# Two graph layers over one streamed adjacency: each engine's order written out call by call, with 12 input checks on VectorE

## The chip, the cores and the metric

The kernel runs on one NeuronCore of one Trainium2 chip. The metric is device time in microseconds, the median over runs of the same program. Beside those runs stands one profiled execution, from which every row below comes; its span starts at the first recorded instruction and ends at the last.

## The reference, cut to what matters

```python
def _L0_gnn_ref(x, adj, W, a):
    Wh = x @ W
    e = leaky_relu((Wh @ a[:128])[:, None] + (Wh @ a[128:])[None, :], 0.2)
    mask = (adj > 0) | eye(4096)
    alpha = softmax(where(mask, e, NEG_INF), axis=1)
    return alpha @ Wh

def _L1_gnn_ref(z, dist_matrix, W, B):
    sens = exp(-(1.0 / dist_matrix - 1.0) ** 2 / 0.5)
    return where(dist_matrix < 1.0, sens, 0.0) @ (z @ W + B)

h = relu(layernorm(x));  x = x + _L0_gnn_ref(h, adj, W0, a0)
h = relu(layernorm(x));  x = x + _L1_gnn_ref(h, adj, W1, B1)
```

`x` is 4096 x 128 and `adj` is 4096 x 4096, both float32, so `adj` is 67 MB. Its entries are 0 or 1 and most are 0; edges are dense only among the first nodes. With entries of 0 and 1 the second layer adds nothing: a 0 gives exp of minus infinity, a 1 fails the cutoff. The kernel relies on that, checks it for every entry, and has a general path (a branch behind a flag) for any other input.

## The kernel before

**Work in chunks.** `adj` is read in 32 chunks of 2 MB (128 partitions x 16384 bytes), numbered 0 to 31. Eight chunks, in two halves of four column blocks, make up one *super* of 1024 rows; there are four supers. The chunks go through a ring of six buffers (`adj_ring`). SyncE issues all loads (line 347); the load of chunk i waits until chunk i - 6 has been packed, has been turned where that is needed, and has been checked (lines 358 to 369).

**What is done to a chunk.**
- *check* (VectorE line 1035, or ScalarE lines 866 and 869): every entry is 0 or 1. `DVE_CHECKED` names the chunks that VectorE checks with one pass (13 of them), `ACT_CHECKED` those that ScalarE checks with two passes (19). Chunk 31 is VectorE's.
- *pack* (TensorE lines 560, 567 and 573): matmuls fold the adjacency bits of eight rows and the column number into one float word in PSUM (`bank`). The two chunks 2n and 2n+1 share *step* n and its PSUM banks. Blocks on the diagonal come from `clean`, written by `clean_diagonal` on VectorE (line 1051).
- *scan* (VectorE line 1065): the largest 8 words of each segment of a packed step go to `cand`, after both chunks of the step are packed.
- *turn_hub*, *turn_columns*, *hub*, *column* handle the first 128 nodes and the first 128 columns, which are dense, with weights for all pairs instead of a list of edges. `add_columns(s)` (TensorE line 670) starts the sums of super s in PSUM.

**Edges.** The 16 steps are cut into five *pieces* (steps 0-3, 4-7, 8-11, 12-14, 15). After the last scan of piece n, VectorE runs `pick(n)` (line 1078 on), TensorE `place(n)` (lines 629 and 636), VectorE `decode(n)` (line 1181 on, node numbers to `index`) and `pick_shared(n)` (line 1108 on), TensorE `place_shared(n)` (line 646), VectorE `decode_shared(n)` (line 1145 on, to `shared_index`). GpSimd then fetches one row of `node_table` per partition and slot with an indirect DMA (line 478), 76 in all, in 11 *groups* g over a ring of four. For each group VectorE computes edge weights with `weigh(g)` (lines 1222 to 1251, to `spread`), and TensorE adds the weighted rows into the sums with `scatter(g)` (line 682). `add_self(s)` (line 677) adds each node itself, scaled beforehand by ScalarE (`scale_self`, line 889). `epilogue(s)` (VectorE lines 1313 and 1319) divides and adds to `x_sb`; SyncE stores it. The sums of all supers use the same PSUM banks, so `add_columns(s)` waits for `epilogue(s - 1)`. `row_scores` (TensorE line 601) and `row_weights` (ScalarE line 878) prepare each super's row factors, in two halves.

**The end.** `judge` (VectorE lines 1335 to 1340) waits for ScalarE's last check and stands ahead of `weigh(10)`; `count_bad` (TensorE line 699) and `raise_flag` (ScalarE line 895) turn the verdicts into the flag. Then `scatter_last` and `last_epilogue` end the kernel in three parts.

**What sets the order.** There is no scheduler: each engine executes its instructions in the order of its block and waits on semaphores. Before the change each block loops over the chunks and takes from tables at which chunk a call is made:

```python
PICK_AT = {8: 0, 16: 1, 24: 2, 30: 3}
WEIGH_AT = {13: 0, 15: 1, 17: 2, 20: 3, 22: 4, 25: 5, 28: 6}
SCATTER_AT = {14: 0, 16: 1, 18: 2, 21: 3, 23: 4, 26: 5, 29: 6, 30: 7}
EPILOGUE_AT = {19: 0, 27: 1}
```

So `scan(n)` stands at chunk 2n + 2 on VectorE, `place(n)` ahead of the pack of the chunk in `PICK_AT`, and so on; the end of VectorE's block is `epilogue(2)`, `scan(15)`, `pick(4)`, `pick_shared(4)`, `decode_shared(4)`, `check(31)`, `weigh(8)`, `weigh(9)`, `judge()`, `weigh(10)`, `last_epilogue()`.

## Time and profile before

| what | us |
|---|---|
| runs of the kernel: median (lowest, highest of 3) | 255.73 (254.72, 261.86) |
| the profiled execution's own time | 253.61 |
| its span | 251.8 |
| busy: TensorE / VectorE / ScalarE / GpSimd | 170.7 / 186.3 / 188.1 / 120.9 |

The profiled execution takes 1.8 us outside its span. In the rows, PE is TensorE's matmuls, DVE is VectorE, ACT is ScalarE, POOL is GpSimd and SP is SyncE; L and a number is the line of the kernel. A number in brackets behind a timeline row is how long the engine sat idle before it, with what ended that wait ("remote" and "issue" name nothing the profile could identify). An f32 matmul is recorded as two instructions, so a `scatter` of 8 matmuls counts x16. The ends of matmuls are modelled, and a few records can be missing.

### The profile page before, as it was taken

How to read it: one execution, taken by the hardware profiler on the slowest of the kernel's cores; microseconds unless marked ns; L12 is line 12 of the kernel's file. 1: busy time of each engine (PE TensorE's matmuls, PEld its weight loads, DVE VectorE, ACT ScalarE, POOL GpSimd, SP SyncE). 2: the span in 40 equal slices, each digit the busy share in tenths (PEclk: the TensorE clock that was granted, in tenths of full speed). 3: DMA queues.
4: the chain of work that ended last, by engine and by line, in shares of the span. 5: the costliest groups of instructions: out<-in, count | busy, mean ns of one | idle time of the engine just before them, and what ended most of it. 6: DMA issues, size and time to landing. Idle time of an engine off the chain costs nothing. (4 is left out here: it accounts for less than half of the span.)

```text
span 251.8 us, 3251 instructions
## 1 busy us (share of the span) xinstructions
PE 170.7 (68%) x970; PEld 118.5 (47%) x970; DVE 186.3 (74%) x563; ACT 188.1 (75%) x201; POOL 120.9 (48%) x131
## 2 busy tenths in 40 slices
PE   0296797595149849794999787557494929557390
PEld 0295553253135525563576554434353626356390
DVE  7967949989988799999599993865317581067963
ACT  0899876977993089899983999999999999900000
POOL 0395040000007798987689898137760027713810
PEclk9999999979557986999599999797887776965778
DMA  5999999999999999999999999999994001120002
GB/s 160 389 410 411 407 410 415 422 411 408 409 409 405 390 394 395 403 394 395 392 393 401 398 391 397 390 408 389 384 392 187 0 5 40 26 85 0 9 10 90
DMA packets 22389, 76.96 MB, mean 306 GB/s; under 512 B 2643, under 2 KB 3255, under 8 KB 22368
## 3 DMA queue, kind: packets, MB, share of 16 engines
q1 hardware_dynamic: 18912, 71.31, 72.5%
q0 software_dynamic: 3040, 5.34, 6.3%
q8 instruction: 9, 0.15, 0.2%
q10 hardware_dynamic: 416, 0.07, 0.2%
q14 instruction: 12, 0.10, 0.1%
HBM read 74.52 MB, written 4.28 MB: 313 GB/s over the span
## 5 line engine op out<-in xcount | busy, mean ns | idle before, releaser
L478 POOL DMA_INDIRECT gathered_rows<-node_table,index x48 | 68.1, 1418 | 73.2 <-issue 45.2
L573 PE MATMUL bank<-adj_ring,pack_w 128*128 128x512 bf16 (+3 forms) x262 | 73.9, 411 | 5.4 <-DVE clean L1051 2.9
L866 ACT ACTIVATE trash_a<-adj_ring,below_one 128x4096 fp8e4<-128x4096 f32 x19 | 70.4, 3705 | 4.3 <-DMA adj_ring<-in_adj 3.3
L869 ACT ACTIVATE trash_a<-adj_ring 128x4096 fp8e4<-128x4096 f32 x19 | 68.7, 3618 | 0.6
L1035 DVE SCALAR_TENSOR_TENSOR trash_v<-adj_ring 128x4096 fp8e4<-128x4096 f32 x13 | 57.3, 4411 | 0.1
L478 POOL DMA_INDIRECT gathered_rows<-node_table,shared_index x28 | 37.7, 1345 | 17.6 <-DVE shared_index L1156 9.4
L573 PEld LDWEIGHTS bank<-adj_ring,pack_w 128*128 128x128 bf16 x262 | 27.3, 107 | 37.7 <-issue 17.6
L682 PE MATMUL bank<-gathered_rows,spread 128*128 128x129 f32 x176 | 27.3, 321 | 8.9 <-DVE spread L1233 8.6
L1065 DVE MAX8 cand<-bank 128x8 f32<-128x120 f32 (+24 forms) x82 | 23.3, 349 | 11.5 <-PE bank L573 8.0
L682 PEld LDWEIGHTS bank<-gathered_rows,spread 128*128 128x128 f32 x176 | 25.9, 233 | 10.2 <-issue 9.9
L895 ACT ACTIVATE bad_terms<-bank 1x48 f32<-1x48 f32 x1 | 0.2, 200 | 22.7 <-PE bank L699 22.7
L878 ACT ACTIVATE r_rows<-bank 128x512 f32<-128x512 f32 x8 | 4.6, 590 | 16.0 <-remote 11.0
L610 PE MATMUL bank<-whe,hub_w 128*128 128x129 f32 x64 | 10.5, 319 | 7.7 <-DVE hub_w L1272 7.3
L560 PE MATMUL bank<-codes,code_w 128*128 128x512 bf16 x32 | 14.2, 445 | 1.8 <-issue 1.8
L1313 DVE RECIPROCAL rden<-bank 128x3 f32<-128x3 f32 (+1 forms) x12 | 2.0, 168 | 16.6 <-remote 16.5
L610 PEld LDWEIGHTS bank<-whe,hub_w 128*128 128x128 f32 x64 | 9.5, 227 | 9.3 <-DVE hub_w L1272 8.8
L835 ACT ACTIVATE spread<-x_sb,shift,rstd 128x128 f32<-128x128 f32 x32 | 13.3, 502 | 0.0
L670 PE MATMUL bank<-hub_whe,col_w 128*128 128x129 f32 x48 | 7.8, 328 | 7.3 <-DVE x_sb L1319 7.3
L629 PE MATMUL bank<-slots,own_lane 128*32 128x8 f32 (+1 forms) x40 | 2.4, 192 | 14.8 <-issue 13.1
L510 PE MATMUL bank<-w_sb,gathered_rows 128*128 128x130 f32 x64 | 10.5, 315 | 1.3 <-ACT whe L849 1.2
L498 PE MATMUL bank<-ident,spread 128*128 128x128 f32 x32 | 6.5, 338 | 6.8 <-ACT spread L835 6.8
L670 PEld LDWEIGHTS bank<-hub_whe,col_w 128*128 128x128 f32 x48 | 7.2, 238 | 7.9 <-issue 7.9
(165 smaller groups left out, 269.9 us busy)
## 6 DMA issues: line engine op xcount, KB each, us to landing
adj_ring<-in_adj SPq DMA_DIRECT2D x32, 2048.0 KB, 18.1
node_table<-whe POOLq DMA_DIRECT2D x4, 532.0 KB, 10.9
x_sb<-in_x SPq DMA_DIRECT2D x8, 256.0 KB, 6.0
out<-x_sb SPq DMA_DIRECT2D x3, 512.0 KB
gathered_rows<-node_table,index POOLq DMA_INDIRECT x48
gathered_rows<-node_table,shared_index POOLq DMA_INDIRECT x28
out<-x_sb SPq DMA_DIRECT2D x2, 192.0 KB
out<-x_sb SPq DMA_DIRECT2D x1, 128.0 KB
```

Of the source, the lines that this page charges most:

```text
L478: pool.indirect_dma_start(out=rows[:, g % RING_GROUPS * GE + t, :], out_offset=None, in_=table, in_offset=bass.IndirectOffsetOnAxis(ap=row ...
L510: last = nc.tensor.matmul(bank[6 + half][:, b * (D + 2):(b + 1) * (D + 2)], hT[:, nb * P:(nb + 1) * P], w0_sb[:, :], start=(b == 0), stop= ...
L560: nc.tensor.matmul(to[:, :], code_w[:, 2 * c + half, :], codes[:, :], start=True, stop=False, skip_group_check=True)
L573: last = nc.tensor.matmul(to[:, lo:hi], pack_w[:, k, :], ring_hi[:, i % AR, row_at + lo:row_at + hi], start=False, stop=(k == KB - 1), ski ...
L610: last = nc.tensor.matmul(bank[7][:, 0:E1], hub_w[:, m % 2, b, :], whe[:, 4 * HUB_ORDER[m] + b, ONE:ONE + E1], start=(m + b == 0), stop=(m ...
L670: last = nc.tensor.matmul(acc_of(t), weights[:, t, :], hub_whe[:, ONE:ONE + E1], start=(t % 3 == 0), stop=True, skip_group_check=True)
L682: return nc.tensor.matmul(acc_of(t), spread[:, g % 2, t * KB:(t + 1) * KB, :], rows[:, g % RING_GROUPS * GE + turn, ONE:ONE + E1], start=F ...
L835: last = nc.scalar.activation(hn_block(b), x_sb[:, b, :], ACT.Identity, bias=shift[:, b:b + 1], scale=rstd[:, b:b + 1])
L866: nc.scalar.activation(trash_a[:, :], ring[:, i % AR, :], ACT.Sign, bias=below_one[:, :], scale=-1.0, accum_out=signs[:, n:n + 1], saturat ...
L869: nc.scalar.activation(trash_a[:, :], ring[:, i % AR, :], ACT.Abs, accum_out=sizes[:, n:n + 1], saturate=False).then_inc(checked_a, 1)
L1035: nc.vector.scalar_tensor_tensor(trash_v[:, :], ring[:, i % AR, :], 1.0, ring[:, i % AR, :], ALU.is_ge, ALU.not_equal, accum_out=bad_v[:, ...
L1065: last = nc.vector.max(cand[:, at * 8:(at + 1) * 8], word_bank(step, half)[:, lo:hi])
```

## The change

The loops and their tables are gone. In their place each engine has a list of calls. The functions are the same but for a few waits: `turn_hub` of every chunk but the first no longer waits for the cleared diagonal; `row_scores(1, ..)` waits for the hub mask; `clean_diagonal` waits only for the packs that read its buffer; a semaphore `self_added` lets an epilogue wait for `add_self`; `pick_shared` waits for the words of `place`. VectorE checks 12 chunks: 7 and 31 go to ScalarE, 24 comes to VectorE, and ScalarE's last checks come in the order 27, 28, 30, 29, 26, 31.

```diff
-DVE_CHECKED = [0, 1, 4, 2, 5, 7, 10, 12, 14, 17, 19, 21, 31]
-ACT_CHECKED = [i for i in range(CHUNKS) if i not in DVE_CHECKED]
+DVE_CHECKED = [1, 0, 2, 4, 5, 10, 12, 14, 17, 19, 21, 24]
+ACT_CHECKED = [3, 6, 7, 8, 9, 11, 13, 15, 16, 18, 20, 22, 23, 25, 27, 28, 30, 29, 26, 31]
...
                 if i:
                     pe.wait_ge(hub_kept, i)
-                if i == CLEARED:
-                    pe.wait_ge(diag_cleared, 1)
+                else:
+                    pe.wait_ge(r_rows_set, 2)
...
                 elif s == 1:
                     pe.wait_ge(col_w_set, 2)
+                    pe.wait_ge(hub_kept, 2 * CC)
                     to = bank[5 + half]
...
             def add_self(s):
                 pe.wait_ge(self_scaled, s + 1)
                 for t in range(KB):
-                    nc.tensor.matmul(acc_of(t), ident[:, :], whe[:, KB * s + t, ONE:ONE + E1], start=False, stop=True,
-                                     skip_group_check=True)
+                    last = nc.tensor.matmul(acc_of(t), ident[:, :], whe[:, KB * s + t, ONE:ONE + E1], start=False,
+                                            stop=True, skip_group_check=True)
+                last.then_inc(self_added, 1)
...
@@ TensorE @@
+            pack(0)
+            turn_hub(0)
+            quad_scores(0)
+            pack(1)
+            pack(2)
+            turn_hub(2)
+            quad_scores(1)
+            pack(3)
+            pack(4)
+            pack(5)
+            turn_columns(4)
+            pack(6)
...
+            place(0)
+            hub_group(2)
+            pack(8)
+            hub_group(3)
+            hub_group(4)
+            pack(9)
+            pack(10)
+            hub_group(5)
+            row_scores(1, 0)
+            pack(11)
+            hub_group(6)
+            row_scores(1, 1)
+            pack(12)
+            hub_group(7)
+            place_shared(0)
+            pack(13)
...
+            pack(24)
+            place(2)
+            pack(25)
+            scatter(4)
+            place_shared(2)
+            pack(26)
+            row_scores(3, 1)
+            scatter(5)
+            pack(27)
+            turn_columns(26)
+            add_columns(2)
+            pack(28)
+            turn_columns(27)
+            pack(29)
+            add_self(2)
+            place(3)
+            pack(30)
+            place_shared(3)
+            scatter(6)
+            pack(31)
+            scatter(7)
             place(4)
             place_shared(4)
-            add_self(SG - 1)
+            add_columns(3)
+            add_self(3)
...
@@ ScalarE @@
+            keep_hub(0)
+            quad_weights()
+            check(3)
+            keep_hub(2)
+            pair_weights()
+            check(6)
+            keep_hub(4)
+            check(7)
+            keep_hub(6)
+            check(8)
+            check(9)
+            check(11)
+            row_weights(1, 0)
+            keep_hub_rows()
+            row_weights(1, 1)
+            scale_self(0)
+            check(13)
+            scale_self(1)
+            check(15)
+            check(16)
+            scale_self(2)
+            row_weights(2, 0)
+            check(18)
+            row_weights(2, 1)
+            check(20)
+            check(22)
+            row_weights(3, 0)
+            check(23)
+            scale_self(3)
+            check(25)
+            row_weights(3, 1)
+            check(27)
+            check(28)
+            check(30)
+            check(29)
+            check(26)
+            check(31)
...
-                if i >= 8:
-                    dve.wait_ge(packed, i - 7 if i % 2 == 0 else i - 7)
+                for old in CLEANED[:CLEANED.index(i)]:
+                    if old % 2 == i % 2:
+                        dve.wait_ge(packed, old + 1)
...
                 dve.wait_ge(merged, n + 1)
+                if LANE_GROUPS[n]:
+                    dve.wait_ge(words_done, n + 1)
...
                 dve.wait_ge(scattered, max(g for g in range(GROUPS) if SUPER_OF_GROUP[g] == s) + 1)
+                dve.wait_ge(self_added, s + 1)
...
@@ VectorE @@
+            check(1)
+            quad_masks()
+            check(0)
+            score_terms()
+            check(2)
+            check(4)
+            scan(0)
+            clean_diagonal(5)
+            clear_diagonal(4)
+            scan(1)
+            own_and_hub_weights()
+            check(5)
+            hub(0)
+            column(4)
+            scan(2)
+            hub(1)
+            clean_diagonal(8)
+            scan(3)
+            pick(0)
+            hub(2)
+            hub(3)
+            column(5)
+            decode(0)
+            hub(4)
+            clean_diagonal(9)
+            hub(5)
+            hub(6)
+            scan(4)
+            check(10)
+            pick_shared(0)
+            hub(7)
+            scan(5)
+            decode_shared(0)
+            check(12)
+            weigh(0)
+            scan(6)
+            column(14)
+            scan(7)
+            column(15)
+            clean_diagonal(16)
+            pick(1)
+            check(14)
+            clean_diagonal(17)
+            pick_shared(1)
+            decode(1)
+            weigh(1)
+            decode_shared(1)
+            scan(8)
+            weigh(2)
+            scan(9)
+            check(17)
+            epilogue(0)
+            check(19)
+            weigh(3)
+            column(20)
+            check(21)
+            column(21)
+            scan(10)
+            scan(11)
+            weigh(4)
+            clean_diagonal(24)
+            pick(2)
+            clean_diagonal(25)
+            pick_shared(2)
+            decode(2)
+            weigh(5)
+            decode_shared(2)
+            check(24)
+            epilogue(1)
+            scan(12)
+            scan(13)
+            column(26)
+            weigh(6)
+            column(27)
+            scan(14)
+            pick(3)
+            decode(3)
+            pick_shared(3)
+            weigh(7)
+            decode_shared(3)
+            scan(15)
+            pick(4)
             epilogue(2)
-            scan(STEPS - 1)
-            pick(4)
             pick_shared(4)
             decode_shared(4)
```

**TensorE, the last packs.** Before, from the turn matmuls of the fourth piece on (`place(3)`'s second half, `place_shared(3)`, `pack(30)`, `add_self(2)`, `scatter(7)`, `pack(31)`, `add_columns(3)`, `place(4)`, `place_shared(4)`, `add_self(3)`):

```order
L636 MATMUL bank<-turn_of_p,placed 128x8
L646 MATMUL bank<-half_of_tq,stats 128x4
L560 MATMUL bank<-codes,code_w 128x512
L573 MATMUL bank<-adj_ring,pack_w 128x512 x4
L560 MATMUL bank<-codes,code_w 128x512
L573 MATMUL bank<-adj_ring,pack_w 128x512 x4
L677 MATMUL bank<-whe,ident 128x129 x8
L682 MATMUL bank<-gathered_rows,spread 128x129 x8
L573 MATMUL bank<-adj_ring,pack_w 128x512 x8
L670 MATMUL bank<-hub_whe,col_w 128x129 x8
L629 MATMUL bank<-slots,own_lane 32x8 x4
L646 MATMUL bank<-half_of_tq,stats 128x4
L677 MATMUL bank<-whe,ident 128x129 x8
```

Now, from the second half of `place(3)`:

```order
L619 MATMUL bank<-turn_of_p,placed 128x8
L542 MATMUL bank<-codes,code_w 128x512
L555 MATMUL bank<-adj_ring,pack_w 128x512 x4
L542 MATMUL bank<-codes,code_w 128x512
L555 MATMUL bank<-adj_ring,pack_w 128x512 x4
L629 MATMUL bank<-half_of_tq,stats 128x4
L666 MATMUL bank<-gathered_rows,spread 128x129 x8
L555 MATMUL bank<-adj_ring,pack_w 128x512 x8
L666 MATMUL bank<-gathered_rows,spread 128x129 x8
L612 MATMUL bank<-slots,own_lane 32x8 x4
L629 MATMUL bank<-half_of_tq,stats 128x4
L653 MATMUL bank<-hub_whe,col_w 128x129 x8
L660 MATMUL bank<-whe,ident 128x129 x8
```

`pack(30)` (L542, L555) stands between the two halves of the placement instead of behind both; `add_self(2)` is gone from here to a place ahead of `place(3)`; `scatter(6)` stands ahead of `pack(31)` (the row of 8 L555) and `scatter(7)` behind it; and the placement of the last piece (L612, L629) stands ahead of `add_columns(3)` (L653).

**VectorE, between the last epilogue but one and the last scan.** Before, from the middle of `epilogue(2)` to the start of `pick_shared(4)`:

```order
L1319 SCALAR_TENSOR_TENSOR x_sb<-bank,rden,x_sb 128x128 x3
L1313 RECIPROCAL rden<-bank 128x2
L1319 SCALAR_TENSOR_TENSOR x_sb<-bank,rden,x_sb 128x128 x2
L1065 MAX cand<-bank 128x8 x4
L1078 TENSOR_REDUCE full<-cand 128x1
L1084 MAX slots<-cand 128x8
L1098 TENSOR_SCALAR full<-slots 128x1
L1108 TENSOR_TENSOR mv<-bank,iota 32x32
L1117 MAX shared_slots<-mv 32x8
L1120 MATCH_REPLACE mv<-shared_slots,mv 32x32
```

Now the same calls:

```order
L1134 MAX cand<-bank 128x8 x4
L1147 TENSOR_REDUCE full<-cand 128x1
L1153 MAX slots<-cand 128x8
L1167 TENSOR_SCALAR full<-slots 128x1
L1385 RECIPROCAL rden<-bank 128x3
L1391 SCALAR_TENSOR_TENSOR x_sb<-bank,rden,x_sb 128x128 x3
L1385 RECIPROCAL rden<-bank 128x3
L1391 SCALAR_TENSOR_TENSOR x_sb<-bank,rden,x_sb 128x128 x3
L1385 RECIPROCAL rden<-bank 128x2
L1391 SCALAR_TENSOR_TENSOR x_sb<-bank,rden,x_sb 128x128 x2
```

`scan(15)` and `pick(4)` (L1134 to L1167) have moved ahead of `epilogue(2)` (L1385, L1391).

**VectorE, behind the last decode.** Before, from `shared_index` of the last piece to the spread of `weigh(8)`:

```order
L1156 TENSOR_TENSOR shared_index<-shared_column,shared_empty 128x4
L1158 TENSOR_TENSOR stats<-shared_i,shared_mask 128x32
L1162 TENSOR_TENSOR std<-shared_lane,lane_number 128x16
L1166 TENSOR_SCALAR stats<-stats 128x32
L1168 TENSOR_TENSOR shared_on<-stats,std 128x128
L1035 SCALAR_TENSOR_TENSOR trash_v,verdicts<-adj_ring 128x4096
L1222 TENSOR_TENSOR edge_w<-r_slots,gathered_rows 128x64
L1225 TENSOR_TENSOR edge_w<-edge_w,gathered_rows 128x64
L1228 TENSOR_TENSOR edge_w<-edge_w,bits_i 128x64
L1233 TENSOR_TENSOR spread<-edge_w,lane_of_p 128x1024
```

Now:

```order
L1227 TENSOR_TENSOR shared_index<-shared_column,shared_empty 128x4
L1229 TENSOR_TENSOR stats<-shared_i,shared_mask 128x32
L1233 TENSOR_TENSOR std<-shared_lane,lane_number 128x16
L1237 TENSOR_SCALAR stats<-stats 128x32
L1239 TENSOR_TENSOR shared_on<-stats,std 128x128
L1293 TENSOR_TENSOR edge_w<-r_slots,gathered_rows 128x64
L1296 TENSOR_TENSOR edge_w<-edge_w,gathered_rows 128x64
L1299 TENSOR_TENSOR edge_w<-edge_w,bits_i 128x64
L1304 TENSOR_TENSOR spread<-edge_w,lane_of_p 128x1024
```

`check(31)` (L1035) has left VectorE's end; `weigh(8)` follows the decode at once.

## Rows read from the trace of the kernel before

**Rows 1.** The page: granted TensorE clock and DMA share, 40 slices of the span.
```profile
PEclk9999999979557986999599999797887776965778
DMA  5999999999999999999999999999994001120002
```

**Rows 2.** Windows of core 0: us, busy by engine, granted clock, DMA share, GB/s.
```profile
35.00:72.00 37.00, 21.28 (x115) 11.42 (x113) 32.90 (x64) 29.77 (x24) 3.00 (x5) 0.82 1.03 413
72.00:190.00 118.00, 92.16 (x546) 60.94 (x546) 89.74 (x238) 100.07 (x86) 84.80 (x60) 0.87 1.02 395
72.00:221.00 149.00, 111.75 (x648) 74.49 (x648) 105.04 (x299) 130.52 (x103) 96.55 (x72) 0.85 0.84 321
190.00:200.00 10.00, 7.34 (x33) 5.50 (x33) 6.99 (x24) 9.78 (x7) 0.00 (x0) 0.66 0.21 83
190.00:252.00 62.00, 36.77 (x195) 29.82 (x194) 35.65 (x134) 30.95 (x21) 20.92 (x16) 0.73 0.13 40
```

**Rows 3.** The page, groups of ScalarE: busy, mean ns, idle before.
```profile
L866 ACT ACTIVATE trash_a<-adj_ring,below_one 128x4096 fp8e4<-128x4096 f32 x19 | 70.4, 3705 | 4.3 <-DMA adj_ring<-in_adj 3.3
...
L878 ACT ACTIVATE r_rows<-bank 128x512 f32<-128x512 f32 x8 | 4.6, 590 | 16.0 <-remote 11.0
```

**Rows 4.** Timeline of ScalarE: start, us, line, operation, count.
```profile
190.50 3.71 ACT L866 ACTIVATE trash_a<-adj_ring,below_one 128x4096 fp8e4<-128x4096 f32 x1
...
220.76 0.19 ACT L869 ACTIVATION_READ_ACCUMULATOR trash_a<-adj_ring 128x1 f32 x1
```

**Rows 5.** Timeline of VectorE, 107 us.
```profile
107.92 4.41 DVE L1035 SCALAR_TENSOR_TENSOR trash_v<-adj_ring 128x4096 fp8e4<-128x4096 f32 x1
```

**Rows 6.** Timeline of VectorE from 192 us; idle time before in brackets.
```profile
192.16 0.61 DVE L1319 SCALAR_TENSOR_TENSOR x_sb<-bank,rden,x_sb 128x128 f32<-128x128 f32 x2
...
220.11 0.18 DVE L1313 RECIPROCAL rden<-bank 128x3 f32<-128x3 f32 x1 [11.49 <-remote]
...
222.30 0.61 DVE L1319 SCALAR_TENSOR_TENSOR x_sb<-bank,rden,x_sb 128x128 f32<-128x128 f32 x2
...
230.19 0.29 DVE L1168 TENSOR_TENSOR shared_on<-stats,std 128x128 f32<-128x128 f32 x1
230.40 4.42 DVE L1035 SCALAR_TENSOR_TENSOR trash_v<-adj_ring 128x4096 fp8e4<-128x4096 f32 x1
...
242.13 0.29 DVE L1222 TENSOR_TENSOR same<-r_pair,gathered_rows 128x128 f32<-128x128 f32 x1 [2.17 <-DMA gathered_rows<-node_table,shared_index]
...
247.13 0.61 DVE L1319 SCALAR_TENSOR_TENSOR x_sb<-bank,rden,x_sb 128x128 f32<-128x128 f32 x2
```

**Rows 7.** Waits of SyncE's queue: total us, times, longest.
```profile
SPq L366 <- DVE trash_v L1035: 52.3, 9, 12.1
```

**Rows 8.** Timeline of TensorE from 176 us.
```profile
176.37 1.06 PE L573 MATMUL bank<-adj_ring,pack_w 128*128 128x512 bf16 x4
...
192.92 3.78 PE L670 MATMUL bank<-hub_whe,hub_w 128*128 128x129 f32 x16 [2.66 <-DVE x_sb L1319]
...
206.82 0.56 PE L646 MATMUL bank<-half_of_tq,stats 32*128 32x4 f32 x2 [4.13 <-DVE stats L1126]
...
207.71 1.91 PE L573 MATMUL bank<-adj_ring,pack_w 128*128 128x512 bf16 x4
...
213.51 1.95 PE L682 MATMUL bank<-gathered_rows,spread 128*128 128x129 f32 x16
...
229.17 3.59 PE L677 MATMUL bank<-whe,ident 128*128 128x129 f32 x16
236.88 6.57 PE L682 MATMUL bank<-gathered_rows,spread 128*128 128x129 f32 x32 [4.13 <-DVE spread L1233]
```

**Rows 9.** Timeline of GpSimd, 230 us and the last.
```profile
230.61 5.08 POOL L478 DMA_INDIRECT gathered_rows<-node_table,shared_index  x1 [9.38 <-DVE shared_index L1156]
...
239.31 1.15 POOL L478 DMA_INDIRECT gathered_rows<-node_table,shared_index  x1 [0.30 <-issue]
```

**Rows 10.** Waits between 190 and 252 us.
```profile
DVE rden L1313 <- remote: 16.5, 2, 11.5
```

271 lines of the change are left out of this document (109 added, 162 removed).

## The prediction, made before the changed kernel ran

> **What bounds the kernel now.** I read the slices of the page first: the reader is to see that the DMA engines are full from the start to 189 us and nearly idle behind it [rows 1]. Up to 190 us the kernel is bound by the stream of adjacency: at 395 to 413 GB/s [rows 2] its 67 MB cannot come sooner whatever the engines' order, as long as a load is always queued. So only the 62 us behind the stream are to be won. There the windows show no full engine but ScalarE: from 190 to 252 us TensorE works 36.8 us and VectorE 35.7 [rows 2]. ScalarE is busy without a break until its last check ends at 220.95 us, one check taking (220.95 - 190.50) / 4 = 7.6 us [rows 4]; `judge` comes after it at once, so ScalarE isn't what ended last.
>
> Then the timelines, backwards. The kernel's tail is a relay between VectorE and TensorE with a backlog of chunks: `pack(30)` is at work at 207.7 us and `pack(31)` comes behind `scatter(7)` of 213.5, 18 and 26 us behind the last landing [rows 8]. Its hand-overs are: `epilogue(1)` ends at 192.8 [rows 6] and releases `add_columns(2)` at 192.9; `place_shared(3)` waits 4.1 us, to 206.8, since VectorE does `weigh(7)` between `place(3)` and the shared pick [rows 8]; `epilogue(2)` waits 11.5 us for `scatter(7)` and ends at 222.9; `scan(15)` and `pick(4)` come only then; the last decode ends at 230.5; `check(31)` takes 4.4 us right behind it; TensorE waits 4.1 us and starts `scatter(8)` at 236.9 [rows 6, 8]; `weigh(10)` starts at 242.1 [rows 6]. From there to the end of the span (251.8) it is 9.7 us, and from the end of `scatter(9)`, 243.5 [rows 8], 8.3 us.
>
> One warning on the rows: `scatter(7)`'s matmuls end at 215.5, but `epilogue(2)`, whose last missing semaphore is theirs, starts at 220.1, and the profile calls the releaser "remote" [rows 6, 8, 10]. The Trainium skill (Perfetto Trace Analysis, Tensor Engine Instruction) says that TensorE's end times are estimated and not observed; the trace agrees, by 4.6 us here. Taking the rows' own ends for the packs and scatters would make the forecast some 4 us lower than it stands. I go by the waiter's start where there is one.
>
> **Prices.** Four 512-column matmuls take 1.06 us at the full clock and 1.91 at the lower of its two levels [rows 8], so a pack of 8 is 2.0 or 3.7 us, the two code matmuls of an even chunk being as wide, 0.5 or 0.9 more; `scatter` 2.0 or 3.3, `add_self` and `add_columns` 2.0 or 3.7 [rows 8]. The granted clock over 72 to 221 us is 0.85 [rows 2], but the tail is at 0.73; I take 3.3 and 2.9 for packs, 2.7 for a scatter, 2.8 for the sums. A check is 4.4 us on VectorE [rows 6], 7.6 on ScalarE.
>
> **Part 1, the stream (0 us).** The order decides when a ring buffer comes free. SyncE already waits 52 us in all for checks of VectorE [rows 7], and these waits cost nothing while another load is queued. Three checks of VectorE move back: `check(14)` now stands behind `pick(1)` and ends by my walk at 121, before at 112.3 [rows 5]; `check(17)` and `check(24)` end at 141 and 181. A chunk passes in 5.2 to 5.8 us, so load 20 must be queued by 122 us, load 23 by 139, load 30 by 178. I expect gaps of 2 or 3 us and a last landing near 192. What hides them is the backlog: `pack(31)` isn't reached before 205. If that cover were gone they would cost their 3 us.
>
> **Part 2, ScalarE (+7.6, not on the path by itself).** It has 20 checks for 19. Its waits of before are 16.0 us at `row_weights` and 4.3 at landings [rows 3]. Now check 7 fills part of the idle time near 70 us, but `keep_hub_rows` waits for the hub sums (about 6 us), `row_weights(2, 0)` for 3, `row_weights(3, 0)` for 6, and chunk 6 lands 5 us after ScalarE is ready: 20 again. The first check starts 3 us sooner. 220.95 + 7.6 - 3 = 225.6 for the last check; `judge` and `weigh(10)` follow at 226.2, which gives a span of 226.2 + 9.7 = 235.9. Behind the last check nothing else queues on ScalarE but the flag.
>
> **Part 3, the backlog at 190 us.** I walked the new lists call by call from 35 us with the prices above. VectorE has the same ten checks up to `epilogue(1)`, and `scan(12)` and `column(26)` now stand behind it. It waits about 23 us: 5 at `decode_shared(0)`, whose `place_shared(0)` stands three packs later on TensorE; 4 at `decode_shared(1)`; the rest at packs and hub sums. `epilogue(1)` ends at 184.7 for 192.8: 8.1 us. The least and the most I can justify: nothing (each wait removed comes back at the hand-over behind it), and 14 (half of the 23 us vanish at the full clock).
>
> **Part 4, between the epilogues.** `add_columns(2)` to 188.1, `pack(28)`, `turn_columns(27)` and `pack(29)` to 194.7, `scan(14)` and `pick(3)` to 197.6, `add_self(2)` and `place(3)` to 198.7. Then, the shared pick no longer behind `weigh(7)`, the 4.1 us wait of `place_shared(3)` goes; it stands behind `pack(30)` (202), whose 3.3 us hide VectorE's pick. `scatter(6)` to 205.2, `pack(31)` 208.1, `scatter(7)` 210.8, `epilogue(2)` 213.8 for 222.9. That is 9.1, so 1.0 more than at `epilogue(1)`: the saved wait is mostly spent on a longer row of matmuls. `weigh(7)` needs its rows: piece 2's 16 fetches start at 171, at some 1.4 us each (1.15 and a pause of 0.30), plus one that is stretched by `check(24)`, as the fetch under `check(31)` took 5.1 us for 1.2 [rows 9]. They land at 199, just in time for 200.8. Bounds of this gain: -3 (the fetches 4 us late) and 5 (the saved wait comes through).
>
> **Part 5, the last piece.** `scan(15)` and `pick(4)` run before `epilogue(2)` in the shade of `scatter(7)`, `place(4)` before `add_columns(3)`. After `epilogue(2)` only the shared pick and the decode are left, 3.0 us: 216.8, where it was 230.5 - 222.9 = 7.6: 4.6 us gained. Then `check(31)`'s 4.4 us are gone from VectorE, but TensorE becomes late in its place: `add_columns(3)` and `add_self(3)` to 221.3 at my price (223 at the low clock), `scatter(8)` and `scatter(9)` to 226.7 (230). I take 228.2, which is 15.3 before the 243.5 of before; so of the 4.4 us only 15.3 - 8.1 - 1.0 - 4.6 = 1.6 come through. Bounds 0 and 4.4. The four fetches for `weigh(10)` start at 216.4 and are in at 224, before ScalarE is done.
>
> **Sum.** 8.1 + 1.0 + 4.6 + 1.6 = 15.3 us. Span 251.8 - 15.3 = 236.5 (ScalarE's own chain gives 235.9), with the 1.8 us outside it 238.3 against 253.61 of the profiled execution. That execution is 2.1 us under the median of the runs, 255.73; I forecast 240.
>
> **Rivals.**
> *Only ScalarE bounds.* If TensorE keeps its full clock and hands over at once, ScalarE's waits shrink from 20 to 10 us; its last check ends at 216, the span 216.6 + 9.7 = 226, the time 228 to 233. For it: TensorE worked only 92 of 118 us between 72 and 190 [rows 2]. Against it: the hub rows can't come before the eighth hub group, behind `pack(12)`.
> *The waits change places.* Words placed a chunk later hold VectorE at the decodes, and each of five decodes and three `finished` waits costs 1 to 2 us: parts 3 and 4 bring nothing and part 5's 6.2 us stay or go: 255.7 - 6.2 = 249.5, up to 256. For it: VectorE's block has no spare work at these places. Against it: before, it stood still 11.5 us in one place.
> *The clock falls, and the kernel is slower.* Packing as chunks land puts a pause behind each pack. From 35 to 72 us TensorE was busy 21 of 37 us and had 0.82; from 190 on, busy 37 of 62, 0.73; 0.87 where it was busy 92 of 118 [rows 2]. Its work from 72 us on is 92.2 x 0.87 + 36.8 x 0.73 = 107 us at the full clock. To end 24 us later than forecast (2% over before) it has 182 us for them: slower from a mean clock of about 0.66 on, with 20 us of waiting. At 0.60 the time is near 265. The Trainium skill (TensorE: Matmul & The Clock Gate, HAM oscillation) warns of this: a loop whose bursts are shorter than its waits for data runs cold in every turn; the trace agrees in direction alone.
>
> **How the numbers follow.** Forecast with its own range 234 to 246: 0.5. Only ScalarE: 0.2. Waits change places: 0.23, most of it within 2%. Clock: 0.07. The range for 8 in 10 is 229 to 253; its ends are the parts at their bounds: 240 - 6 (part 3) - 4 (part 4) = 230, with a little of part 5's; 240 + 8 + 4 + 2 = 254, less than all at once. About 2% can be told from no change: faster by more (under 250.6) 0.77, within 0.16, slower (over 260.8) 0.07.
>
> **What would show it.** Right: `epilogue(1)` ends near 185 and `epilogue(2)` near 214; no wait of 4 us at the last `place_shared`; `scan(15)` ahead of `epilogue(2)`; `judge` and `scatter(9)` within 3 us of each other, ScalarE's last check at 223 to 228; DMA share 9 to 192 us. Wrong: `epilogue(1)` still after 190, a gap in the DMA share before 180 with `pack(31)` waiting for its landing, or a mean granted clock under 0.7.

## The result, and the profile after

The changed kernel takes 232.44 us (median of 4 runs, 232.01 to 233.31), the kernel before, run beside it, 256.97 us: ratio 0.908 [0.899, 0.916]. The forecast was 240. The measured time is 1.6 us under the forecast's own range (234 to 246) and inside the range for 8 in 10 (229 to 253). Ratios, here and below, compare each kernel's fast runs, so they differ a little from the ratio of the medians.

That ratio holds for the chip of this measurement. In the experiments below the kernel before took 233.8, 234.8 and 235.0 us on three other chips, and 259.0 on a fourth. Where it takes 235, the changed kernel takes 230.1: ratio 0.980 [0.974, 0.985]. So the change is worth 4.7 us where the kernel before takes 235 us, and 24.5 us where it takes 257, and the text has to explain both. The profiled execution after took 232.01 us, its span 230.2.

The page of the changed kernel: slices, then groups of line, engine and operation (busy, mean ns, idle before):

```profile
PEclk9999999979795999788799799996799797976978
DMA  5999999999999999999999999999999993130002
...
L903 ACT ACTIVATE trash_a<-adj_ring,below_one 128x4096 fp8e4<-128x4096 f32 x20 | 74.1, 3706 | 8.3 <-DMA adj_ring<-in_adj 7.6
L1103 DVE SCALAR_TENSOR_TENSOR trash_v<-adj_ring 128x4096 fp8e4<-128x4096 f32 x12 | 53.0, 4417 | 1.4 <-DMA adj_ring<-in_adj 1.3
```

And of its groups on ScalarE:

```profile
L915 ACT ACTIVATE r_rows<-bank 128x512 f32<-128x512 f32 x8 | 4.7, 594 | 4.8 <-PE bank L584 4.8
```

The stream of loads is as it was [rows 1]: the DMA share is 9 up to the 33rd slice, which ends at 190 us. ScalarE has one check more. It waits 4.8 us at `row_weights` where it waited 16.0, and 8.3 instead of 4.3 ahead of its checks (7.6 and 3.3 of that for landings) [rows 3].

Windows of the changed kernel (us, busy by engine, granted clock, DMA share, GB/s):

```profile
35.00:72.00 37.00, 25.66 (x140) 14.44 (x141) 33.03 (x78) 31.01 (x28) 3.01 (x5) 0.86 1.03 412
72.00:190.00 118.00, 92.88 (x555) 61.47 (x563) 97.61 (x254) 110.14 (x92) 86.89 (x58) 0.89 1.03 395
190.00:230.20 40.20, 25.50 (x153) 21.30 (x154) 23.50 (x105) 27.69 (x19) 18.80 (x18) 0.81 0.19 60
```

From 72 to 190 us ScalarE works 10 us more and VectorE 8 us more than in [rows 2]; behind 190 us TensorE has 25.5 us left instead of 36.8, VectorE 23.5 instead of 35.7 (4.4 of VectorE's 12.2 are `check(31)`, which left it). The backlog shrank. The clock did not fall: behind 190 us it is 0.81, before 0.73.

VectorE of the changed kernel, against [rows 6] (start, us, line, operation, idle before in brackets):

```profile
177.03 0.61 DVE L1391 SCALAR_TENSOR_TENSOR x_sb<-bank,rden,x_sb 128x128 f32<-128x128 f32 x2
...
193.45 0.17 DVE L1252 CAST words_i<-bank 128x8 int32<-128x8 f32 x1 [2.33 <-remote]
...
201.66 0.18 DVE L1385 RECIPROCAL rden<-bank 128x3 f32<-128x3 f32 x1
...
207.34 0.29 DVE L1239 TENSOR_TENSOR shared_on<-stats,std 128x128 f32<-128x128 f32 x1
...
217.63 0.18 DVE L1408 SCALAR_TENSOR_TENSOR excess<-sizes,signs 128x20 f32<-128x20 f32 x1 [2.75 <-issue]
217.93 0.18 DVE L1413 TENSOR_SCALAR verdicts<-excess 128x20 f32<-128x20 f32 x1
218.04 0.29 DVE L1293 TENSOR_TENSOR same<-r_pair,gathered_rows 128x128 f32<-128x128 f32 x1
```

`epilogue(1)` ends at 177.6 and `epilogue(2)` starts at 201.66 without a wait; before, it waited 11.5 us to 220.11. `decode_shared(4)` ends at 207.6. Then VectorE runs ahead of ScalarE, whose last check ends at 217.6:

```profile
213.89 3.62 ACT L906 ACTIVATE trash_a<-adj_ring 128x4096 fp8e4<-128x4096 f32 x1
217.41 0.19 ACT L906 ACTIVATION_READ_ACCUMULATOR trash_a<-adj_ring 128x1 f32 x1
```

`judge` (the `excess` row) follows at once and `weigh(10)` behind it. TensorE no longer sets `weigh(10)`'s start.

### The profile page after: what moved, and what is told of

It reads as the page before. It is cut to its first block, busy times and chain, and to the rows that moved or that the text cites. A ratio compares the mean times of both kernels' runs of the same rounds, so it can differ in the third digit from the quotient of the medians.

```text
span 230.2 us, 3246 instructions
## 1 busy us (share of the span) xinstructions
PE 163.5 (71%) x957; PEld 113.0 (49%) x970; DVE 182.1 (79%) x561; ACT 195.2 (85%) x205; POOL 122.0 (53%) x131
## 4 chain that ended last, share of the span: by engine, by line
DMA 32%; PE 25%; issue 14%; ACT 14%; DVE 9%; SPq 2%; POOL 2%; another core or an unknown queue 1%; DVEq 0%; POOLq 0%; ACTq 0%
DMA adj_ring<-in_adj 29%; PE bank L555 9%; PE bank L666 7%; ACT trash_a L903 7%; ACT trash_a L906 6%; DVE trash_v L1103 4%; DMA gathered_rows<-node_table,index 2%; PE bank L660 2%; POOL gathered_rows L460 2%; PE bank L653 2%; SPq L337 2%; PE bank L542 1%; PE bank L699 1%; DVE x_sb L1391 1%
## 5 line engine op out<-in xcount | busy, mean ns | idle before, releaser
L460 POOL DMA_INDIRECT gathered_rows<-node_table,index x48 | 72.9, 1518 | 56.5 <-issue 43.0
L903 ACT ACTIVATE trash_a<-adj_ring,below_one 128x4096 fp8e4<-128x4096 f32 x20 | 74.1, 3706 | 8.3 <-DMA adj_ring<-in_adj 7.6
L555 PE MATMUL bank<-adj_ring,pack_w 128*128 128x512 bf16 (+3 forms) x255 | 74.1, 421 | 9.7 <-DMA adj_ring<-in_adj 5.5
L906 ACT ACTIVATE trash_a<-adj_ring 128x4096 fp8e4<-128x4096 f32 x20 | 72.3, 3617 | 0.6
L1103 DVE SCALAR_TENSOR_TENSOR trash_v<-adj_ring 128x4096 fp8e4<-128x4096 f32 x12 | 53.0, 4417 | 1.4 <-DMA adj_ring<-in_adj 1.3
L555 PEld LDWEIGHTS bank<-adj_ring,pack_w 128*128 128x128 bf16 x262 | 27.2, 108 | 42.1 <-issue 17.8
L460 POOL DMA_INDIRECT gathered_rows<-node_table,shared_index x28 | 32.8, 1172 | 8.5 <-issue 8.5
L1134 DVE MAX8 cand<-bank 128x8 f32<-128x120 f32 (+24 forms) x82 | 23.1, 350 | 7.0 <-PE bank L555 7.0
L542 PE MATMUL bank<-codes,code_w 128*128 128x512 bf16 x26 | 11.3, 436 | 9.6 <-issue 5.1
L492 PEld LDWEIGHTS bank<-w_sb,gathered_rows 128*128 128x128 f32 x64 | 9.2, 221 | 2.6 <-ACT gathered_rows L878 2.4
L612 PE MATMUL bank<-slots,own_lane 128*32 128x8 f32 (+1 forms) x40 | 2.4, 193 | 10.7 <-ACT hub_mask L894 6.0
L1339 DVE TENSOR_SCALAR hub_w<-r_hub,whe 128x128 f32<-128x128 f32 x32 | 8.9, 346 | 1.3 <-PE bank L593 1.3
L542 PEld LDWEIGHTS bank<-codes,code_w 128*128 128x128 bf16 x32 | 3.7, 115 | 12.6 <-issue 8.7
L943 ACT ACTIVATE whe<-whe,w_self 128x129 f32<-128x129 f32 x32 | 9.8, 391 | 0.0
L1391 DVE SCALAR_TENSOR_TENSOR x_sb<-bank,rden,x_sb 128x128 f32<-128x128 f32 x32 | 9.4, 346 | 0.4
```

Of the source, the lines that this page charges most:

```text
L460: pool.indirect_dma_start(out=rows[:, g % RING_GROUPS * GE + t, :], out_offset=None, in_=table, in_offset=bass.IndirectOffsetOnAxis(ap=row ...
L492: last = nc.tensor.matmul(bank[6 + half][:, b * (D + 2):(b + 1) * (D + 2)], hT[:, nb * P:(nb + 1) * P], w0_sb[:, :], start=(b == 0), stop= ...
L542: nc.tensor.matmul(to[:, :], code_w[:, 2 * c + half, :], codes[:, :], start=True, stop=False, skip_group_check=True)
L555: last = nc.tensor.matmul(to[:, lo:hi], pack_w[:, k, :], ring_hi[:, i % AR, row_at + lo:row_at + hi], start=False, stop=(k == KB - 1), ski ...
L903: nc.scalar.activation(trash_a[:, :], ring[:, i % AR, :], ACT.Sign, bias=below_one[:, :], scale=-1.0, accum_out=signs[:, n:n + 1], saturat ...
L906: nc.scalar.activation(trash_a[:, :], ring[:, i % AR, :], ACT.Abs, accum_out=sizes[:, n:n + 1], saturate=False).then_inc(checked_a, 1)
```

## Is the time before the order's or the chip's?

**The same two kernels again, on another chip.** Nothing edited.

> The kernel before, unchanged. On the occasion of the first four experiments it took 233.8 us, where it took 257 us when it was first set beside the changed kernel. Theory: the 23 us are not the order's; in the first measurement this kernel lost them in its tail behind 190 us, where TensorE's granted clock was 0.73 and its semaphores came late. Then its profile here ends near 232 us with the loads' last landing at 190 us again, epilogue(1) within 3 us of 192.8, but epilogue(2) 8 to 12 us earlier than 222.9 and a mean granted clock above 0.8 behind 190 us. Rival: the loads came later in the first measurement; then epilogue(1) is earlier here by 15 us or more. Rival 2: it is a matter of the chip, and this run gives 255 us again.

> The changed kernel, unchanged. Theory: beside the kernel before on the same chip and occasion it takes 230.5 to 233 us, a ratio of 0.985 to 1.0, since new_head and new_tail gave 0.999 and 0.987 there. Rival: its gain of 9% comes back, with the kernel before at 255 us; then what makes the kernel before slow hits only its own order.

Measured: before 234.82 us, ratio to itself 1.001 [0.997, 1.004]; changed 230.08 us, 0.980 [0.974, 0.985]. VectorE of the kernel before on this chip, against [rows 6]:

```profile
179.34 0.18 DVE L1313 RECIPROCAL rden<-bank 128x3 f32<-128x3 f32 x1 [0.76 <-PE bank L682]
...
181.53 0.61 DVE L1319 SCALAR_TENSOR_TENSOR x_sb<-bank,rden,x_sb 128x128 f32<-128x128 f32 x2
...
203.97 0.18 DVE L1313 RECIPROCAL rden<-bank 128x3 f32<-128x3 f32 x1 [7.49 <-PE bank L682]
...
212.12 4.42 DVE L1035 SCALAR_TENSOR_TENSOR trash_v<-adj_ring 128x4096 fp8e4<-128x4096 f32 x1
...
223.79 0.29 DVE L1222 TENSOR_TENSOR same<-r_pair,gathered_rows 128x128 f32<-128x128 f32 x1 [2.10 <-DMA gathered_rows<-node_table,shared_index]
```

The loads end at 190 to 192 us on both chips, on this one if anything later, so the rival with later loads is out. My theory was right that the time is lost in the tail, and wrong on where it starts: `epilogue(1)` is 10.6 us earlier here already, not within 3. `epilogue(2)` is 16.1 earlier (I had said 8 to 12), the end of the span (233.1) 18.7. The two waits that ended with "remote" [rows 10] end here with TensorE's L682, by name and at once.

**What TensorE does there.** In the first profile `scatter(7)` was modelled to end at 215.46 and its waiter went on at 220.11 [rows 6, 8]. Here its rows are

```profile
201.98 1.95 PE L682 MATMUL bank<-gathered_rows,spread 128*128 128x129 f32 x16
```

that is, to 203.93, and the waiter starts at 203.97. I matched every release of a TensorE semaphore that the traces hold (some 130 each) with the modelled end of its matmul. On the chips of 235 us none comes more than 0.3 us late, in ten profiles. On the other kind it happens in all four profiles, by up to 5.7 us in the kernel before, 8 in the changed one, and 10 or more in the two with added matmuls. The rows themselves show it in the changed kernel's first profile, in `scatter(8)` (16 matmuls) with `scatter(9)` behind it:

```profile
212.38 0.94 PE L666 MATMUL bank<-gathered_rows,spread 128*128 128x129 f32 x7
214.34 0.27 PE L666 MATMUL bank<-gathered_rows,spread 128*128 128x129 f32 x1 [1.02 <-issue]
215.76 0.36 PE L666 MATMUL bank<-gathered_rows,spread 128*128 128x129 f32 x1 [1.15 <-issue]
217.87 4.38 PE L666 MATMUL bank<-gathered_rows,spread 128*128 128x129 f32 x23 [1.74 <-issue]
```

Matmuls of `scatter(8)`, which wait for nothing inside the call, start 1.4 to 2.1 us apart. The same call on the other chip is one row, without a pause:

```profile
210.50 3.74 PE L666 MATMUL bank<-gathered_rows,spread 128*128 128x129 f32 x32
```

So on one kind of chip something holds TensorE for microseconds at a time, and the granted clock hardly shows it: the changed kernel's mean is 0.885 there and 0.905 here, that of the kernel before 0.846 and 0.880. For the kernel before, the window from 190 to 228 us has 0.74 there and 0.82 here; on its 24 us of matmuls that is an estimated 2 us, worked out from these two numbers, of the 18.7. The page "Perfetto Trace Analysis" of the Trainium skill (Tensor Engine Instruction) says why this is hard to see: TensorE's ends are estimates. What holds it stays open.

**Who pays for it.** Both kernels are held, but compare each with itself on the two chips, VectorE first chip against second. Before: `epilogue(1)` +10.6, `epilogue(2)` +16.1, end +18.7; the lateness grows from landmark to landmark. Changed: `epilogue(1)` +0.3, `decode(3)` +2.3 (193.45 for 191.16), `epilogue(2)` +0.8, `judge` +0.0 (217.63 for 217.60), end +1.8. Two readings fit. One is slack: `add_columns(3)` was released 8 us late (217.9 for 209.9) and `judge` not a bit later. The other is that the holds fell elsewhere: in the kernel before, late releases crowd between 172 and 190 us (`scatter(5)`, which `epilogue(1)` waits for, by 5.6 us), and in the changed kernel there is none over 0.3 us for matmuls that end between 132 and 183 us, so its `epilogue(1)` had little to take up. To try the first, I added TensorE's own work at known places.

## Experiments on TensorE's lateness

**Four packs twice.** In either kernel, in `pack(i)`:

```diff
+                for again in range(2 if h == 0 and i >= 24 else 1):
                     for half in range(2):
```

> The kernel before, with the matmuls of pack(24), pack(26), pack(28) and pack(30) done twice: TensorE is later by 2.2 us (full clock) to 4.2 us (low clock) at four places behind 160 us, about 12 us in all, as it was late in the first profile of this kernel (5.5 us at scatter(5), 4.6 at scatter(7), 5.7 at pack(31)). Theory: the first measurement's 23 us more than here are TensorE's lateness passed on by the old order: this run is 8 to 12 us slower than the kernel before (243 to 247 us). Rival: TensorE has slack in the old order and the 23 us came from elsewhere: 0 to 4 us slower.

> The changed kernel with the same four packs done twice. Theory: the new order takes up TensorE's lateness where the old one passes it on, since scatters and sums stand well behind their weights and ScalarE's checks bound the end: only 1 to 6 us slower than the changed kernel's 230.1, 231 to 236 us. Rival: both orders pass it on alike, 8 to 12 us, 238 to 242 us; then the first measurement's ratio of 0.908 stays without a cause in the order.

Measured: before 239.19 us, ratio 1.023 [1.017, 1.030], by the ratio +5.5 us (4.2 between the medians); changed 232.68, 0.992 [0.989, 0.995] for 0.980, +2.8 us (2.6 between the medians, which come from two chips). The old order passes on less than my theory said (8 to 12), and the new order about half of that. In the changed kernel `epilogue(2)` was 6.7 us later (207.61 for 200.91) and the span only 2.4 longer. ScalarE's last check ended 3.3 us later (220.9 for 217.6), and `judge` still waited 2.8 us for it where it had waited 5.6: that wait took up the rest.

**Two packs four times.** The same line with `range(4 if i in (26, 30) else 1)`.

> The kernel before, with the matmuls of pack(26) and pack(30) done four times: 6.6 us (full clock) to 12.6 us (low clock) more of TensorE's work at each of the two places where its semaphores were 4 to 6 us late in the first profile. Doing pack(24), (26), (28) and (30) twice cost 5.5 us of some 12. Theory: two long stalls hit what the backlog doesn't cover: 10 to 18 us slower, 245 to 253 us. Rival: the half that passed before passes again, 6 to 9 us, 241 to 244 us.

> The changed kernel with pack(26) and pack(30) done four times. Doing four packs twice cost it 2.8 us. Theory: it has some 4 us of slack in the tail (judge waits 5.6 us for ScalarE) and otherwise passes on the same stalls: 5 to 12 us slower, 235 to 242 us, a ratio to before_two_stalls of 0.94 to 0.97, so that lateness at these places explains part of the first measurement's 0.908 and not all. Rival: the ratio falls to 0.92 or under (the new order is all of it); rival 2: above 0.975 (it explains nothing).

These two happened to run on a chip of the slow kind: the kernel before took 258.99 us there. Measured: before with stalls 266.29 us, ratio 1.026 [1.011, 1.042], +7 us; changed with stalls 240.68, ratio 0.936 [0.925, 0.947]. Against the first measurement's 0.908 that is some 7 or 8 us for the changed kernel, if this chip is like that one: the changed kernel without stalls did not run beside it. So stalls of 7 to 12 us cost both orders about alike, within wide intervals: the slack took up part of the short lateness and nothing that shows of the long. The ratio between the two is 0.91 (0.936 over 1.026), which is the rival's and not the 0.94 to 0.97 of the theory. But without any added stall it was 0.908, so the added stalls did not make it. This pair doesn't show that the order's slack is what keeps the chip's own holds out.

The holds show in this profile of the kernel before (an execution of 270.6 us, where the median was 266.3) more plainly than anywhere, inside one `scatter`. It stands at 127 us, ahead of both added stalls:

```profile
127.36 0.41 PE L683 MATMUL bank<-gathered_rows,spread 128*128 128x129 f32 x2 [1.06 <-issue]
128.81 0.27 PE L683 MATMUL bank<-gathered_rows,spread 128*128 128x129 f32 x1 [1.05 <-issue]
129.52 0.57 PE L683 MATMUL bank<-gathered_rows,spread 128*128 128x129 f32 x1 [0.43 <-issue]
```

That call's rows begin at 124.4 us and reach 135.6, where a scatter takes 2 to 3.8 us when it is not held.

## Experiments on the parts of the change

All on chips where the kernel before takes 234 to 235 us. The expectations of `new_head`, `new_tail`, `c31_on_dve` and `no_check31` were written when only the 257 us of the first measurement were known, so they are read by their ratios. All six are edits of the changed kernel: where they have the old order, they keep the few changed waits.

**Head and tail of the order apart.** `new_head` has the new lists up to chunk 23 and the old order from `pack(24)`, `scale_self(3)` and `clean_diagonal(24)` on. `new_tail` is the reverse.

```diff
 new_head
+DVE_CHECKED = [1, 0, 2, 4, 5, 10, 12, 14, 17, 19, 21, 31]
 new_tail
+DVE_CHECKED = [0, 1, 4, 2, 5, 7, 10, 12, 14, 17, 19, 21, 24]
```

> The new order up to chunk 23 on all three engines, the old order behind it (with check 31 back at VectorE's end; check 24 on ScalarE; 12 checks on VectorE). Theory 1, the gain is the backlog that the new head removes: epilogue(1) ends near 178 us as in the changed kernel (192.8 before), the old tail adds its own relay, 257 - 15 = 242 us. Rival, the gain sits in the order of the tail: 248 us or more.

> The old order up to chunk 23, the new order behind it (13 checks on VectorE: 7 in the head, 24 in the tail, none at the end). Theory 1 (backlog from the head): epilogue(1) ends after 188 us and only the 6 us of the tail come through, 251 us. Rival (tail order): 242 us or less, since the crossings of the engines in the tail were what held the old kernel.

Measured: `new_head` 233.90 us, 0.999 [0.992, 1.006]; `new_tail` 231.47, 0.987 [0.982, 0.993]. The head alone brings nothing, the opposite of my theory, which gave it the larger part: the backlog that it removes doesn't set the end as long as the old tail follows. The tail brings 1.3% and the whole 2.0%; `new_tail` also has `check(31)` on ScalarE, so it isn't the tail's order alone. Its profile, one of its fastest executions, has `epilogue(2)` and `weigh(10)` each 2.7 us sooner than the kernel before; in the median nothing of that is left.

**check(31) on either engine, in either order.** `c31_on_dve` is the changed kernel with the check back on VectorE; `old_c31_on_act` has the old order and the check last on ScalarE.

```diff
 c31_on_dve (VectorE; check(31) goes from ScalarE's list)
             decode_shared(4)
+            check(31)
             weigh(8)
 old_c31_on_act (ScalarE; check(31) goes from VectorE's list)
             check(30)
+            check(31)
```

> The changed kernel with check 31 on VectorE behind decode_shared(4), as before the change; ScalarE then has 19 checks. Theory 1: VectorE has idle time there (2.3 us at weigh(9), 2.8 us at judge) and ScalarE is done 7.6 us sooner, so it costs 0 to 2 us: 232 to 235. Rival, a check at the end costs its own 4.4 us and stretches the fetches of the last groups by 4 us: 237 to 240, with weigh(9) starting after 216.

> The order of before in every list, but check(31) last on ScalarE instead of behind decode_shared(4) on VectorE; 20 checks on ScalarE, 12 on VectorE. Theory: ScalarE's last check ends at 224.7 (217.1 in the second profile of before, and 7.6), 3 us behind the place where judge stood (221.2); VectorE is 4.4 us sooner at weigh(8), and the end goes by judge: 234 to 237 us, no gain, so the check can move only once the order has made ScalarE earlier. Rival: the check's move alone is most of the gain, as c31_on_dve beside the changed kernel (0.992 and 0.980 of before) suggests: 231 to 232 us.

| ratio to before | check(31) on VectorE | on ScalarE |
|---|---|---|
| old order | 1 | 1.018 [1.014, 1.022] |
| new order | 0.992 [0.987, 0.997] | 0.980 [0.974, 0.985] |

In microseconds `c31_on_dve` took 232.40 and `old_c31_on_act` 238.35. The cells come from three chips, each as a ratio to the kernel before on the same chip. Checks 7 and 24 change engines with the order, and the upper right cell has the changed waits, the upper left not. By the ratios, moving the check by itself costs 4.3 us, the order by itself brings 1.9, both together 4.7. Neither part is the gain; the order is worth 9 us once the check has moved (1.018 to 0.980). With the check back on VectorE the changed kernel loses 2.9 us, between my theory (0 to 2) and the rival (5 or more). In the old order ScalarE, with 20 checks, ends at 223.9 and VectorE waits for it:

```profile
223.89 0.18 DVE L1408 SCALAR_TENSOR_TENSOR excess<-sizes,signs 128x20 f32<-128x20 f32 x1 [7.76 <-ACT trash_a L906]
```

`weigh(10)` starts at 224.29, only 0.5 us behind the quiet profile of before. The rest comes behind it: TensorE, which waited 6.1 us at `count_bad`, runs `scatter_last` at its lower clock, 3.78 us for 2.02. I had put the run at 234 to 237 and it took 238.35. With the new order, on the second chip, ScalarE's 20 checks end 6.3 us sooner: between 31 us and its last check it waits 13.8 us there and 19.4 here. Its waits at `hub_w` (5.4 us) are gone and those at `row_weights` halved (6.6 to 3.1), while those at landings rise (3.8 to 9.3).

And with the check on VectorE it isn't its 4.4 us on VectorE that set `weigh(10)`, but what happens to the fetches under it, GpSimd of `c31_on_dve`:

```profile
207.90 5.21 POOL L460 DMA_INDIRECT gathered_rows<-node_table,shared_index  x1 [0.30 <-issue]
213.41 1.62 POOL L460 DMA_INDIRECT gathered_rows<-node_table,shared_index  x1 [0.30 <-issue]
...
217.97 1.00 POOL L460 DMA_INDIRECT gathered_rows<-node_table,shared_index  x1 [0.30 <-issue]
```

One fetch takes 5.21 us for 1.0, the last is issued at 217.97 instead of 212.54 in the changed kernel on its second chip, and `weigh(10)` waits for it:

```profile
220.66 0.29 DVE L1292 TENSOR_TENSOR same<-r_pair,gathered_rows 128x128 f32<-128x128 f32 x1 [2.81 <-DMA gathered_rows<-node_table,shared_index]
```

**How much ScalarE's last check costs.** `no_check31` leaves out the check of chunk 31's values altogether.

```diff
-            check(31)
```

> The changed kernel without the check of chunk 31 (left out; ScalarE has 19 checks). Theory 1, ScalarE is not the bound, the fetches of the last group (in at 217.9) and TensorE are: 232, within 1 us. Rival, ScalarE's last check (ends 217.5) bounds the end, or what it does holds TensorE's signals back until 217.9: 225 to 228, with add_columns(3) released near 210.

Measured: 228.71 us, 0.975 [0.969, 0.981]. Against the changed kernel's 0.980 that is 1.1 us, inside the intervals, and between my theory (232) and the rival (225 to 228). The profile doesn't price the check: `weigh(10)` starts at 218.03, as in the changed kernel (218.01), and now waits 2.4 us for its fetches. But these fetches run 2.9 us later than in the changed kernel's quiet profile, since the words of piece 3 came later (193.65 for 191.16), ahead of anything that the edit touches. So how far the fetches are behind ScalarE's check differs from execution to execution, between 0 and 2.5 us in these profiles. What the span gains (1.0 us) is in `scatter_last`, 2.02 us for 3.45, as below.

**A version that waits less.** `late_judge` takes `judge` and `count_bad` out from ahead of the last group:

```diff
             weigh(9)
-            judge()
             weigh(10)
+            judge()
...
-            count_bad()
             scatter_last()
+            count_bad()
```

> The changed kernel with judge behind weigh(10) on VectorE, and count_bad behind scatter_last on TensorE. Theory: in the changed kernel's second profile judge waits 5.6 us for ScalarE's last check and count_bad holds TensorE 3.9 us, so that weigh(10) starts at 219.0 though its rows are there about 216; the new place gives 2 to 3 us, 227 to 228.5 us. Rival: weigh(10) waits for its fetches until 218.5 to 219 anyway, as it did without check(31): 229.5 to 230.5 us.

Measured: 228.36 us, 0.973 [0.969, 0.977], the lowest median of all, 1.5 us under the changed kernel by the ratios. That is 0.6% between two chips, and the two intervals overlap, so it isn't clear of noise. Both sides were half right: `judge` no longer bounds, and now the fetches do.

```profile
217.96 0.29 DVE L1293 TENSOR_TENSOR same<-r_pair,gathered_rows 128x128 f32<-128x128 f32 x1 [2.71 <-DMA gathered_rows<-node_table,shared_index]
...
220.56 0.17 DVE L1408 SCALAR_TENSOR_TENSOR excess<-sizes,signs 128x20 f32<-128x20 f32 x1
```

Fetches run in one unbroken row, most of them one per 1.3 us, from the words of piece 3 on; the last is issued at 215.43, 2.9 us later than in the changed kernel's quiet profile, and `weigh(10)` starts at the same 218.0 all the same (ScalarE's last check ends at 218.84 here). And TensorE doesn't stand at `count_bad` before the last group. `scatter_last` of the changed kernel there, and of `late_judge`:

```profile
218.13 0.25 PE L683 MATMUL bank<-verdicts,one_column 128*1 128x48 f32 x2 [3.90 <-DVE verdicts L1413]
219.83 3.45 PE L666 MATMUL bank<-gathered_rows,spread 128*128 128x129 f32 x16 [1.45 <-DVE spread L1322]
```

```profile
219.78 2.02 PE L666 MATMUL bank<-gathered_rows,spread 128*128 128x129 f32 x16 [2.35 <-DVE spread L1322]
```

The 1.4 us between 3.45 and 2.02 are the clock's: in the changed kernel it is at its lower level (0.50) from 219.8 to 221.6 us and at 0.65 to 223.3, behind the 3.9 us wait; in `late_judge` it is 1.00.

## Why the prediction was right or wrong

The landmarks, in us of the span. "Quiet" is the chip of the second profiles.

| | forecast | changed, first | changed, quiet | before, first | before, quiet |
|---|---|---|---|---|---|
| `epilogue(1)` ends | 184.7 | 177.6 | 177.3 | 192.8 | 182.1 |
| `epilogue(2)` ends | 213.8 | 204.4 | 203.7 | 222.9 | 206.8 |
| last decode ends | 216.8 | 207.6 | 206.8 | 230.5 | 212.2 |
| ScalarE's last check ends | 225.6 | 217.6 | 217.6 | 220.95 | 217.3 |
| `weigh(10)` starts | 226.2 | 218.0 | 218.0 | 242.1 | 223.8 |
| span | 236.5 | 230.2 | 228.4 | 251.8 | 233.1 |

**Part 1, the stream: right.** No gap in the DMA share; `check(14)` ended at 115.7, `check(24)` at 174.9, sooner than I walked. SyncE's wait for VectorE's checks rose from 52.3 us [rows 7] to

```profile
SPq L348 <- DVE trash_v L1103: 57.5, 7, 14.9
```

at no cost.

**Part 2, ScalarE: the step that failed.** "20 again" for its waits was 12.7: 4.8 at `row_weights`, 7.6 at landings, 0.3 at the hub masks. With these 7.3 us less my 225.6 becomes 218.3, and it was 217.6. Two things were mis-sized. 11.0 of the 16.0 us at `row_weights` were "remote" [rows 3]; releases of `row_scores` came 4.3 and 4.8 us behind their modelled ends near 82 us, and on the quiet chip, where none is late, the kernel before waits 6.7 there. And `keep_hub_rows`, for which I set 6 us, waited for nothing.

**Part 3, the backlog: 15.2 us for 8.1,** and more than the most that I could justify (14; by its own words, half of 23 us on top of 8.1, that bound should have been 19.6). My walk of the new list was 7 us slow, and the 192.8 from which I subtracted held 10.6 us of the chip's. On the quiet chip the order brings 4.8 us here.

**Part 4, between the epilogues.** I forecast 29.1 us from one to the other, and it took 26.8 (26.4 quiet), for 30.1 before; but on the quiet chip the kernel before needs only 24.7, so the step loses 1.7 us there. The wait for `scatter(7)` was 7.5 us there and gone, as forecast, but the row of matmuls is longer. The 4.1 us wait at `place_shared(3)` went, and one of 3.6 came at `place_shared(4)`, which I hadn't listed (1.3 there before): `place(4)` is now done before `epilogue(2)`, and the shared pick only behind it.

```profile
205.61 0.58 PE L629 MATMUL bank<-half_of_tq,stats 32*128 32x4 f32 x2 [3.60 <-issue]
```

**Part 5, the last piece: right.** 3.2 us from `epilogue(2)` to the last decode for 3.0, and 7.6 before: 4.4 gained for 4.6. On the quiet chip it is 5.4 to 3.1, 2.3 gained. The sum of the three parts there is 4.8 - 1.7 + 2.3 = 5.4 us at the last decode.

**The end: the wrong bound.** TensorE and ScalarE were to be within 3 us of each other, at 226 to 228. ScalarE's last check set `weigh(10)`, at 218: the rival "only ScalarE bounds", to which I gave 0.2, with its last check at 216 and 228 to 233 us, fits, at 217.6 and 232.4 us. Its condition does not: TensorE did not hand over at once on the first chip. Nor was ScalarE quite alone there. The last fetch was issued at 215.05:

```profile
215.05 1.00 POOL L460 DMA_INDIRECT gathered_rows<-node_table,shared_index  x1 [0.30 <-issue]
```

In the three profiles in which `weigh(10)` waits for that fetch it starts 2.5 to 2.7 us behind its issue, which gives an estimated 217.6 here: the fetches and ScalarE's check were level. On the quiet chip ScalarE bounds by 2.5 us. From `weigh(10)` to the end I carried over 9.7 us; it took 12.2 on the first chip, since `scatter(8)` was held and `scatter(9)` ended at 222.2, behind the weights of the last group (221.0), and 10.4 on the quiet one. So 240 us was 7.6 too high: 8.2 from ScalarE's end (226.2 for 218.0), 1.9 from what I added to its chain (0.6 in the span, 1.3 for the median above the profiled execution), less 2.5 for the slower end. The clock rival and the one in which waits change places are out. (One sum of the clock rival is off: by its own terms, 107 us at 0.60 and 20 of waiting are 198 us where it has 182, so the time would be near 277 and not 265.)

That 240 came this near is in part luck. The forecast gave the order a gain of 15.7 us, and 24.5 were measured, on a chip where the kernel before takes 22 us more than elsewhere; on a quiet chip the same change brought 4.7 us. The same working from a quiet base would have promised far too much.

**What the forecast could not know** is that its base, 251.8, was 18.7 us above the same kernel's span on a quiet chip. The warning stood in the rows: releases called "remote" at two epilogues and at `row_weights`, one of them 4.6 us behind the modelled end. I used it to choose which start to go by, and didn't ask whether another execution would have it.

## What to carry to other kernels

When waiters start microseconds behind the modelled end of their matmuls and the releaser has no name, profile the same kernel on another chip before pricing its tail: here that is 22 of 257 us in the old order, and 2 of 232 in the new.

A check moved off a critical engine and the order that makes room for it are one change: apart they brought -4.3 and +1.9 us, together +4.7 us. Try the two-by-two table before calling either the cause.

Once one bound goes, look at the next: at the end of this kernel ScalarE's last check, `judge` and the fetches lie within 3 us, so each further edit there is worth little.
